# Two attention layers on one core: how queries and keys are split and carried, and in which order the work between the layers stands

## The reference

```python
# layer 0
f = xf @ wf + bf; g = xf @ wg + bg; hh = xf @ wh + bh
s = jnp.einsum('bnk,bmk->bnm', g, f)
attn = jax.nn.softmax(s, axis=-1)
o = jnp.einsum('bnm,bmc->bnc', attn, hh)
x = gamma * o.reshape(b, h, w, c) + x
# layer 1
q = (jnp.einsum('bhwc,cf->bhwf', x, Wq) + bq).reshape(b, n, c)
k = (jnp.einsum('bhwc,cf->bhwf', x, Wk) + bk).reshape(b, n, c)
v = (jnp.einsum('bhwc,cf->bhwf', x, Wv) + bv).reshape(b, n, c)
energy = jnp.einsum('bic,bjc->bij', q, k)
attn = jax.nn.softmax(energy, axis=-1)
out = jnp.einsum('bmn,bmc->bnc', attn, v)    # summed over the rows m
out = gamma * out.reshape(b, h, w, c) + x
```

## Time and profile before

| | us |
|---|---|
| median of 3 runs | 4300.55 |
| the three runs | 4293.32, 4300.55, 4301.33 |
| the profiled execution, its own time | 4295.39 |
| its span, from the first instruction to the last | 4293.3 |
| busy in it: PE, DVE, ACT, POOL | 4051.4, 3335.8, 3116.0, 1953.2 |
| mean granted clock of TensorE | 0.973 of full speed |

### The profile page before, as it was taken

One profiled execution on the slowest core, in us unless ns is written; L12 is line 12 of the kernel. 1 busy time (PEld: TensorE's weight loads), 2 busy tenths in 40 slices (PEclk: granted clock), 3 DMA queues, 4 the chain that ended last, 5 costly groups with the idle time before them and its releaser, 6 DMA issues.

```text
span 4293.3 us, 84333 instructions
## 1 busy us (share of the span) xinstructions
PE 4051.4 (94%) x25628; PEld 1346.7 (31%) x25628; DVE 3335.8 (78%) x6400; ACT 3116.0 (73%) x5594; POOL 1953.2 (45%) x909
## 2 busy tenths in 40 slices
PE   5998999999999999999999999999999999999999
PEld 2223332233322333223332233323332233322333
DVE  6777877778777787778877788777887778877787
ACT  0566986679766797668966689666895668956688
POOL 3795008940189202981039710596106951079500
PEclk6899999999999999999999999999999999999999
DMA  0001000000000000000000000001000010000100
GB/s 32 1 1 31 1 11 1 11 21 1 11 1 11 21 1 11 1 13 18 1 11 1 19 12 1 11 1 31 1 1 12 1 31 1 1 11 1 31 1 11
DMA packets 15055, 41.83 MB, mean 10 GB/s; under 512 B 4068, under 2 KB 4068, under 8 KB 12260
## 3 DMA queue, kind: packets, MB, share of 16 engines
q1 hardware_dynamic: 14692, 36.96, 2.8%
HBM read 20.17 MB, written 8.39 MB: 7 GB/s over the span
## 4 chain that ended last, share of the span: by engine, by line
PE 79%; DVE 9%; issue 7%; ACT 2%; DVEq 0%; SPq 0%; POOL 0%; DMA 0%; ACTq 0%; POOLq 0%
PE sum_banks L494 20%; PE sum_banks L600 20%; PE score_banks L588 20%; PE score_banks L480 11%; PE sum_banks L516 3%; DVE tile_max L924 3%; PE sum_banks L452 2%; DVE o_tr L1107 2%; ACT e_whole L813 1%; DVE c_stack L967 1%; ACT g_tr L739 1%; DVE g_tr L919 1%; DVE k_low L987 0%; DVE x_mid L1150 0%; DVE f_tr L919 0%
## 5 line engine op out<-in xcount | busy, mean ns | idle before, releaser
L813 ACT ACTIVATE e_whole<-score_banks,exp_bias,down 128x512 f32<-128x512 f32 x2048 | 1573.6, 773 | 243.1 <-DVE o_tr L1107 200.3
L356 POOL TENSOR_TENSOR e_sum<-e_sum,e_whole 128x1024 f32<-128x1024 f32 x704 | 1658.9, 2356 | 176.0 <-ACT e_whole L757 131.7
L757 ACT ACTIVATE e_whole<-score_banks,no_bias,down 128x1024 f32<-128x1024 f32 x1024 | 1229.4, 1204 | 666.0 <-PE score_banks L480 633.1
L924 DVE TENSOR_REDUCE tile_max<-sum_banks 128x1 f32<-128x512 f32 (+1 forms) x2128 | 1362.7, 686 | 446.3 <-PE sum_banks L452 439.9
L1107 DVE TENSOR_SCALAR_CACHE_REDUCE o_tr<-score_banks,neg_down 128x1024 f32<-128x1024 f32 x1024 | 1313.1, 1283 | 308.5 <-PE score_banks L588 265.7
L494 PE MATMUL sum_banks<-e_whole,proj 128*64 128x512 f32 x4096 | 1143.2, 636 | 0.0
L600 PE MATMUL sum_banks<-e_whole,v_scaled 128*64 128x512 f32 x4096 | 1058.9, 598 | 51.1 <-DVE v_scaled L1097 19.9
L588 PE MATMUL score_banks<-k_high,q_split 128*64 128x512 f16 x4096 | 802.8, 384 | 42.9 <-ACT e_whole L813 22.0
L588 PE MATMUL score_banks<-k_low,q_split 128*64 128x512 f16 x4096 | 793.4, 379 | 0.0
L353 POOL TENSOR_TENSOR e_sum<-e_whole 128x1024 f32<-128x1024 f32 x32 | 75.4, 2357 | 1538.6 <-ACT e_whole L757 1538.6
L452 PE MATMUL sum_banks<-f_tr,g_tr 33*128 33x512 f16 x2128 | 709.5, 404 | 49.4 <-DVE tile_max L924 45.9
(11 more groups left out here) (154 smaller groups left out, 1721.4 us busy)
## 6 DMA issues: line engine op xcount, KB each, us to landing
x_in<-in_x_dram SPq DMA_DIRECT2D x19, 1024.0 KB, 4.9
out_dram<-x_mid SPq DMA_DIRECT2D x32, 256.0 KB, 2.7
k_high<-k_high SPq DMA_DIRECT2D x32, 128.0 KB, 2.2
k_low<-k_low SPq DMA_DIRECT2D x32, 128.0 KB, 2.2
w<-in_L_conv_wg_dram SPq DMA_DIRECT2D x2, 2.0 KB
w<-in_L_conv_wf_dram SPq DMA_DIRECT2D x2, 2.0 KB
w<-in_L_conv_wh_dram SPq DMA_DIRECT2D x2, 16.0 KB
b<-in_L_conv_bh_dram SPq DMA_DIRECT2D x1, 32.0 KB
```

The costliest lines, as they stand in the source:

```text
L356: nc.gpsimd.tensor_tensor(acc, acc, e_whole[:, i % U0, :], ALU.add).then_inc(e_added, 1)
L757: nc.scalar.activation(e_whole[:, i % U0, :].rearrange("p (a n) -> p a n", a=2), score_banks[:, 2 * (i % 2):2 * (i % 2) + 2, :], ACT.Exp, ...
L813: nc.scalar.activation(e_whole[:, u, h * BANK:(h + 1) * BANK], score_banks[:, 2 * (u % 2) + h, :], ACT.Exp, bias=exp_bias[:, u:u + 1], sca ...
L924: nc.vector.reduce_max(tile_max[:, blk, j:j + 1], sum_banks[:, (2 + j % banks) % 4, :], AX_X).then_inc(a_used, 1)
```

## The change

Four things are changed, all between the layers and in the first rounds of layer 1.

1. For the first three chunks one `high` and one `low` cover all 128 partitions and write q's and k's part together into `k_high` and `k_low`. For the fourth chunk q and k keep operations of their own, as before.
2. SP carries q's parts from there to `q_split` by two DMAs for each chunk, and only when these have landed copies k's parts over them.
3. PE's order between the layers: the last values and the sums of layer 0 stand before most of the transposes and projections, the third projection goes to `pair_b`, and both projections of v move behind the scores of steps 1 and 2. The first scores wait for their own chunk alone and no longer for the low part of the third.
4. In the first rounds of layer 1 the work for the image after the next one is a step later or more, the fourth `project0` stands in round 1, ACT makes the high parts of the fourth chunk behind the exponentials of step 0, and the pieces of f and g on DVE spread over rounds 1 and 2.

```diff
@@ SP
-                for j in range(NCH):
+                for j in range(NCH - 1):
                     cols = slice(j * CH, (j + 1) * CH)
-                    for part, done in ((k_high, high_done), (k_low, low_done)):
-                        sp.wait_ge(done, 2 * (image * NCH + j + 1))
-                        sp.dma_start(part[0:C, cols], part[C:P, cols]).then_inc(k_copied[j], 16)
+                    moved = (image * (NCH - 1) + j + 1) * 16
+                    sp.wait_ge(high_done, image * SPLITS + j + 1)
+                    sp.dma_start(q_split[0:C, cols], k_high[0:C, cols]).then_inc(q_moved, 16)
+                    sp.wait_ge(low_done, image * SPLITS + j + 1)
+                    sp.dma_start(q_split[C:P, cols], k_low[0:C, cols]).then_inc(q_rest_moved, 16)
+                    sp.wait_ge(q_moved, moved)
+                    sp.dma_start(k_high[0:C, cols], k_high[C:P, cols]).then_inc(k_copied[j], 16)
+                    sp.wait_ge(q_rest_moved, moved)
+                    sp.dma_start(k_low[0:C, cols], k_low[C:P, cols]).then_inc(k_copied[j], 16)
+                cols = slice((NCH - 1) * CH, N)
+                sp.wait_ge(high_done, (image + 1) * SPLITS)
+                sp.dma_start(k_high[0:C, cols], k_high[C:P, cols]).then_inc(k_copied[NCH - 1], 16)
...
@@ PE, between_scores: what stands behind the scores of step u
...
                     elif u == 1:
-                        pe.wait_ge(low_done, 2 * (image * NCH + 2))
-                        project_v(1, pair_c)
+                        pe.wait_ge(low_done, image * SPLITS + 2)
+                        project_v(0, pair_c)
                     elif u == 2:
+                        pe.wait_ge(low_done, (image + 1) * SPLITS)
+                        project_v(1, pair_d)
+                    elif u == 3:
                         pe.wait_ge(x_loaded, 16 * loads(ahead))
-                        pe.wait_ge(low_done, 2 * (image * NCH + 4))
-                        turn_x(0, x_in, 0, pair_d[:, 0, :])
-                        turn_x(0, x_in, 1, pair_d[:, 1, :])
...
@@ ACT
...
-                q_high(image, par, 0, pair_b)
-                k_first(image, par, 0, pair_b)
+                high(image, par, 0, pair_b, k_high, slice(0, P))
+                copy_values0(image, NCH - 1)
                 turned_x(image, 2, pair_a[:, 0, :])
...
+                        if first and u == 0:
+                            high(image, par, 3, pair_d, q_split, slice(0, C))
+                            high(image, par, 4, pair_d, k_high, slice(C, P))
...
@@ DVE
...
-                q_low(image, par, 2, pair_a)
-                k_rest(image, par, 2, pair_a)
+                low(image, par, 1, pair_c, k_low, k_high, slice(0, P), slice(0, P))
+                low(image, par, 2, pair_b, k_low, k_high, slice(0, P), slice(0, P))
                 turned_x(image, 1, 3, pair_d[:, 0, :])
...
-                        if second and u == 0:
+                        if second and u == 3:
                             fg_bias(image + 2, par)
-                        if second and u == 4:
+                        if third and u == 0:
                             fg_scales(image + 2)
                             fg_scaled(image + 2, par)
-                        if second and u == 7:
+                        if third and u == 4:
                             fg_rest(image + 2, par)
```

119 lines of the change are left out of this document (57 added, 62 removed).

## The result

| | before | after |
|---|---|---|
| median, us | 4298.23 (4 runs) | 4400.3 (4 runs, 4397.55 to 4402.06) |
| the profiled execution | 4295.39 | 4397.55 |
| its span | 4293.3 | 4395.7 |
| mean granted clock of TensorE | 0.973 | 0.951 |

The ratio is 1.0238, with a 95% interval of 1.022 to 1.0256. The forecast was 4325 in a range of 4306 to 4342. The sign was right, the size was far off: 102 us instead of 24.

A forecast was written before the change was run, and what follows sets the result against it. TensorE, busy 4051.4 of 4293.3 us, was taken to bound the kernel. Its added waits, 3.0 us for each of 8 images, summed to 24 us; on the median of 4300.55 that gave 4325, range 4306 to 4342.

The forecast's parts named there:

- Part 1: Three chunks of four: merging saves 3.4 us of high parts on ACT, 3.9 of low parts on DVE.
- Part 2: SP's queue: two more DMAs per chunk, two landings in series, each taken as 2.2 us.
- Part 3: Between the layers: first scores 3.0 us sooner, TensorE's waits up to there down from 1.27 to 0.26.
- Part 4: Behind the first scores: waits of 1.82, 1.42 and later 2.17 us; head start gone by step 1.
- Rival (a): Transitions: TensorE's clock falls in four to eight images, 1.65 us each, giving 4332 to 4338; chance 0.14.
- Part 5: DVE's f and g pieces later: small operations slower beside POOL's stacking; waits of steps 20 to 24 from 0.44 to 3.58.
- (b): Steps 8 and 20 to 24: loss absorbed where a neighbour waits anyway, 4295 to 4305; chance 0.13.
- (c): Step 1: head start of 1.5 us lasts if the fourth chunk's high parts are ready early, 4289; chance 0.07.
- (d): SP's two serial landings: DMAs land late, at 3.5 to 4.9 us, giving 4343 to 4368; chance 0.06.
- The sum: First transpose of x_mid to step 32: TensorE's waits 14.0 us before, 17.0 after; 3.0 more per image, 24 in all.

The follow-up runs named there:

- b_merge: Kernel before with only the merged high and low parts of the first three chunks and their DMAs, all orders as before: 4289.48 us, ratio 0.9975.
- c_best_late: Kernel after, early first scores kept, work behind them mostly ordered as before, last two project0 behind steps 6 and 7: 4305.8 us, ratio 1.0010 to before.
- a_fill_gate: Kernel after with unread matmuls in TensorE's two waits behind the first scores and POOL's bias_h held behind v_scaled of row 4: 4310.02 us, ratio 1.0015 to before.
- a_fill: Kernel after with matmuls nobody reads filling TensorE's two waits behind the first scores: 4362.16 us, ratio 1.0119 to before.
- a_gate: Kernel after with POOL's bias_h waiting until DVE has made v_scaled of row 4: 4344.42 us, ratio 1.0094 to before.
- b_fg: Kernel before with only DVE's pieces of f and g moved to steps 11, 16 and 20: 4343.07 us, ratio 1.0089.

## Why the prediction was wrong, step by step

**Part 1, the merged operations: right.** One operation of 128 partitions takes what one of 64 took. ACT, then DVE, of after:

```profile
371.23 1.11 ACT L790 ACTIVATE k_high<-score_banks,b1s 128x1024 f16<-128x1024 f32 x1
```

```profile
372.57 1.28 DVE L997 SCALAR_TENSOR_TENSOR k_low<-score_banks,b1s,k_high 128x1024 f16<-128x1024 f32 x1
```

Before it was 1.11 and 1.29. b_merge shows that this, with its DMAs, is worth 0.25% by itself.

**Part 2, the DMAs: right, but for the spread.** The page has the same median landing for the new copies as for the old ones:

```profile
k_high<-k_high SPq DMA_DIRECT2D x32, 128.0 KB, 2.2
...
q_split<-k_high SPq DMA_DIRECT2D x24, 128.0 KB, 2.2
q_split<-k_low SPq DMA_DIRECT2D x24, 128.0 KB, 2.3
```

The two serial landings are what TensorE waited for ahead of the scores of step 1, in after as in c_best_late. Chunk 1's copy of q's low part landed in 2.2 in four images of after and in 2.6 to 3.1 in the other four, which makes the 2.10 to 2.59 of the wait out of 1.70.

**Part 3, the first scores: right, and too low.** 3.8 us sooner (14.90 to 11.09), where 3.0 was worked out; the waits up to there are 0.45, worked out as 0.26. It changed little: DVE's low parts and `x_tr` stand ahead of the reduction of step 0, which came at 374.36, 13.4 us from the first transpose, where it was 16.0.

**Part 4, what follows them: right in its waits, wrong in what they bring.** The two waits were given as 1.82 and 1.42, together 3.24; they are 1.38 and 1.70 to 2.59, together 3.4 in the mean of the eight images, and the second is for the DMA, as worked out. Step 1 was given at 20.9, about the same as before; it is at 20.0. The fourth projection's wait was given as 2.17 and is 1.69. With both other causes taken away (a_fill_gate) step 8 stands 0.7 ahead of before in the mean, where 0.75 was worked out, but that agreement is luck, since the mean holds the falls that were left: the images without a fall are 1.3 ahead. Steps 8 to 24 take 2.5 us longer than before, where the prediction's waits make it 2.7. The whole shift is 1.9 us for an image, 1.2 without a fall, where the sum said 3.0. So the layout of engines and queues had the right sign and size within 2 us; what it left out is that it was made at one clock throughout. One of its terms, the 1.33 from the start of a reduction until ACT sees it, stands in no row; after has 1.31 (374.36 to 375.67).

**Rival (a), the falling clock, was the first cause; its chance and its price were wrong.** The mechanism was named, with its place and its reason, and given 0.14 and 1.65 us for an image, because one image of before had shown a fall of 3.4 us. The runs: all eight images, 10.2 to 17.1 us behind the first scores, and 4.0 us of each image (after against a_fill), 4.6 by the pair a_gate against a_fill_gate. The step that failed is the use of the seven undisturbed transitions as evidence against it. Their waits ahead of the first scores are 0.66 and 0.81; after has 1.38 and at least 1.70 with 1.13 us of work between. The one fall of before followed waits of 0.66 and 0.81 too, so it should have counted for (a) much more than the seven against it. The 1.70 that they stood is one wait by itself, 36.6 us from the first transpose, and it brought no fall in any image of before; a wait of that length brought one in three images of b_merge and in four of after. So no length of a single wait decides it here. The length of the one fall, 3.4 us, was taken for falls behind waits twice as long. The Trainium skill's sentence on short idles between groups of matmuls (TensorE: Matmul & The Clock Gate, A second HAM failure mode: psum-queue depth-cycling) was put there as the argument for a likelier fall. The runs side with it.

**Part 5, the pieces of f and g: the largest error.** The place was right (waits of steps 20 to 24 rise), the price wasn't. I priced the overlap with POOL from the earlier trace rows, 1.13 for a `v_scaled` beside POOL's stacking against 0.42, as if DVE's operation were slowed. It isn't slowed, it is held until POOL's instruction ends: all 32 `v_scaled` of over 0.8 us in before, after, b_fg and a_gate end 0.28 or 0.29 us behind the end of the POOL instruction beside which they started. So its time depends on the length of *POOL's* instruction. The stacking's are about 1.0 each, hence 1.13. Behind the stacking stands `bias_h` with one instruction of 4.5 us, which the prediction doesn't mention at all. In before the `v_scaled` of that row started ahead of it. These are POOL's rows of before:

```profile
422.99 2.03 POOL L331 TENSOR_TENSOR g_stack<-fg_low,ones_h 128x512 f16<-128x512 f16 x2
424.98 4.78 POOL L336 TENSOR_TENSOR proj<-proj,b 128x2048 f32<-128x2048 f32 x1
```

The weights there ran from 424.17 to 425.30, 0.28 past the end of the last stacking instruction (425.02), which `bias_h` follows; and the next row's weights came at 432.30, when `bias_h` had been over since 429.76. Before missed the collision by 0.8 us. The sum of Part 5, +3.1 us for steps 20 to 24, should have been the length of `bias_h`, some 4.2 more than a free `v_scaled`, plus what a wait of TensorE of over 5 us does to its clock. Measured: 6.5 us for an image (after against a_gate), 7.1 (a_fill against a_fill_gate), 5.7 in b_fg.

The Trainium skill has this rule (SBUF — State Buffer, Who interferes with whom): a DVE instruction with two inputs in SBUF contends with a GpSimd instruction that reads SBUF, and whichever comes first makes the other block altogether. The trace agrees in both directions: DVE held in after (4.61), b_fg (4.61) and a_fill (4.60 and more), and, where a `v_scaled` of before was running when `bias_h` started, POOL held for a little: 4.77 to 4.78 in those four images, 4.59 to 4.60 in the other four. The 0.41 of a_gate is a `v_scaled` with no POOL instruction beside it. I hadn't weighed that page against row 6, and with it the price would have been read from POOL's longest instruction.

**Rivals (b), (c) and (d)** did not come about. (c) had its deciding point right: the high parts of the fourth chunk started at 377.20 in after, behind the exponentials. c_best_late put them ahead, and then met a wait for the DMA and a low clock instead; the step from 20.0 to 18.9 at step 1 brought nothing.

**The sum.** Predicted 3.0 us for an image, measured 13.0. Of these a_fill_gate keeps 1.9, and 11.1 are the two causes: the clock behind the first scores 4.0 and the blocked `v_scaled` with the clock behind it 7.1, or 4.6 and 6.5, by which one is taken away first.

What stays open: why the clock in a_fill and a_fill_gate still fell behind the first scores in one image of eight, and in a_gate stayed up in one of eight, with the same instructions, and why a copy of 128 KB, 2.2 us at the median, took up to 3.25 in after and 3.83 in c_best_late. The 2.5 us that steps 8 to 24 lose in a_fill_gate weren't divided further; the waits for projection copies and for `v_scaled` are in it.

## What to carry to other kernels

Price a new wait of the matrix engine by what its clock does afterwards as well: here 3 to 4 us of waits, harmless to the schedule, cost 4 to 5 us of slower matmuls, so put independent work between two groups that wait for each other. When work moves on VectorE or GpSimd, lay their SBUF instructions of both engines beside each other with their lengths, and ask which long one a short one can fall behind. A change made of several parts can hold gains and losses at once; here the merged operations, and two projections put one step later than before, gave 0.7% together, while the whole lost 2.4%. And where the profile names what ended a wait, check in the code that the instruction waits for it: here ACT was named for a wait that the DMA ended.
